# Softmax sums divided untransposed in groups of eight heads, the maxima's product outside the ring of banks, the shared expert's gate product in place

## The reference, cut to what matters

```python
# 16 heads of 16 channels; qc from x, kc and vc from the context
y  = softmax(causal(q @ k.T * scale)) @ v          # self attention
y += softmax(qc @ kc.T * scale) @ vc               # cross attention, added
x  = x + tanh(g0) * (y @ Wp + bp)                  # q, k, v, qc from layernorm(x)
h  = layernorm(x)
out = shared_expert(h) + sum over top 2 of 7 experts of w[e] * expert_e(h)
x  = x + tanh(g1) * out                            # expert: (silu(h @ g.T) * (h @ u.T)) @ d.T
```

## Time and profile before

| | µs |
|---|---|
| median of three runs (lowest, highest) | 1413.26 (1413.21, 1413.28) |
| the profiled execution | 1413.27 |
| its span, first to last instruction | 1411.5 |
| TensorE busy in the span | 1368.6 |
| VectorE busy | 880.9 |
| ScalarE busy | 727.3 |
| GpSimd busy | 365.4 |

### The profile page before, as it was taken

The page is one execution under the profiler, slowest core; times in us unless marked ns, Lnnn a source line. Parts: engine busy times, 40 slices in busy tenths (PEclk is TensorE's granted clock), DMA queues, the critical chain, the costliest instruction groups (busy, mean ns, idle before and its releaser), DMA issues.

```text
span 1411.5 us, 27301 instructions
## 1 busy us (share of the span) xinstructions
PE 1368.6 (97%) x7688; PEld 694.0 (49%) x7689; DVE 880.9 (62%) x1804; ACT 727.3 (52%) x1107; POOL 365.4 (26%) x743
## 2 busy tenths in 40 slices
PE   7988999999999999999999999989999999999997
PEld 4544333333333333333333333364556777777775
DVE  6776888888888888888888888653532222222221
ACT  4644667677777676767676767732210222222221
POOL 5655222222222222222222222200001232233232
PEclk9999999999999999999999999999999999999999
DMA  8754111111111111111111111057004122112111
GB/s 246 237 186 154 43 53 51 48 50 48 47 49 50 51 50 50 49 48 48 48 51 51 50 49 50 7 218 297 0 1 134 26 33 34 30 30 37 30 30 23
DMA packets 57711, 98.43 MB, mean 70 GB/s; under 512 B 7441, under 2 KB 42001, under 8 KB 56657
## 3 DMA queue, kind: packets, MB, share of 16 engines
q1 hardware_dynamic: 50384, 88.10, 18.8%
q0 software_dynamic: 7296, 9.97, 4.5%
HBM read 69.20 MB, written 28.58 MB: 69 GB/s over the span
## 4 chain that ended last, share of the span: by engine, by line
PE 88%; DMA 2%; DVE 2%; ACT 1%; issue 1%; POOL 1%; SPq 0%; POOLq 0%; ACTq 0%; DVEq 0%
PE ps L669 19%; PE ps L834 13%; PE ps L651 13%; PE ps L551 13%; PE ps L847 7%; PE ps L786 5%; PE ps L797 3%; PE ps L718 3%; PE ps L654 2%; PE ps L565 2%; PE ps L858 2%; DMA k_parts<-work 2%; PE ps L555 1%; PE ps L592 1%; PE ps L625 1%
## 5 line engine op out<-in xcount | busy, mean ns | idle before, releaser
L1242 DVE TENSOR_REDUCE mx<-ps 128x1 f32<-128x512 f32 (+1 forms) x832 | 515.1, 662 | 99.6 <-PE ps L551 69.3
L993 ACT ACTIVATE arena<-ps 128x1024 f32<-128x1024 f32 (+1 forms) x512 | 484.3, 995 | 138.7 <-PE ps L651 135.2
L669 PE MATMUL ps<-arena 128*32 128x512 f32 (+5 forms) x2432 | 290.9, 525 | 0.6 <-ACT arena L993 0.4
L551 PE MATMUL ps<-arena 96*128 96x512 bf16 x768 | 263.0, 382 | 7.3 <-DMA arena<-k_parts 2.9
L651 PE MATMUL ps<-arena 98*128 98x512 bf16 x832 | 264.4, 381 | 5.0 <-DMA arena<-rowst 4.9
L1144 POOL TENSOR_SCALAR_AFFINE_SELECT arena<-arena 128x128 f32<-128x128 f32 x256 | 74.8, 292 | 439.2 <-ACT arena L993 429.3
L834 PE MATMUL ps<-arena,work 128*128 x608 | 186.4, 460 | 0.6 <-issue 0.6
L551 PEld LDWEIGHTS ps<-arena 96*128 96x128 bf16 x768 | 74.1, 96 | 178.0 <-DVE mx L1242 103.2
L1520 DVE TENSOR_TENSOR work<-work,ps 128x352 f32<-128x352 f32 x76 | 39.6, 521 | 179.1 <-ACT work L1061 179.1
L834 PEld LDWEIGHTS ps<-arena,work 128*128 128x128 f32 x608 | 112.5, 190 | 57.4 <-issue 1.1
L1242 DVE TENSOR_REDUCE mneg<-ps 128x2 f32<-128x512 f32 (+2 forms) x192 | 112.4, 640 | 23.9 <-PE ps L561 23.4
(11 more groups left out here) (161 smaller groups left out, 1406.8 us busy)
## 6 DMA issues: line engine op xcount, KB each, us to landing
arena<-in_experts SPq DMA_DIRECT2D x8, 2176.0 KB, 12.2
arena<-k_parts SPq DMA_DIRECT2D x64, 198.1 KB
arena<-k_parts SPq DMA_DIRECT2D x64, 132.1 KB
arena<-q_parts SPq DMA_DIRECT2D x64, 96.0 KB
k_parts<-work SPq DMA_DIRECT2D x16, 300.0 KB, 5.2
q_parts<-work SPq DMA_DIRECT2D x12, 384.0 KB, 5.4
arena<-k_parts SPq DMA_DIRECT2D x64, 66.0 KB
arena<-q_parts SPq DMA_DIRECT2D x64, 64.0 KB
```

Of the source, the lines that this page charges most:

```text
L551: mm = pe.matmul(out, qx[:, qt * P:(qt + 1) * P], ks[0:KROWS, T + j * CHUNK:T + (j + 1) * CHUNK], start=True, stop=True)
L669: mm = pe.matmul(ps[32 * q:32 * q + VW, 6, b0:b1], vst[0:kn, r % VR, TT + kt if cross else kt, :], pr[0:kn, c0:c0 + b1 - b0], start=(phase ...
L993: act.activation(pr[:, c0:c0 + n], ps[:, 2 * (g % 2):2 * (g % 2) + 2, :].rearrange("p b n -> p (b n)")[:, 0:n], ACT.Exp, scale=SCALE).then ...
L1242: return dve.tensor_reduce(m, out, AX_X, ALU.max)
```

## The change

Three things are done.

- **Sums.** `norm`, `norm_out`, `cross_sums` and `head_output` are gone. After `sums_out`, SyncE stores the sums of each head to memory (`sums_store`, 256 KB). For each group of eight heads it loads the denominators spread over 128 partitions (`den_load`), and the numerators of eight heads stacked over 128 partitions (`num_load`), which is already the channels-first layout that the projection reads (`yT`, in the place of `xnT`). GpSimd adds (`den_sums`, `num_sums`), VectorE takes one reciprocal, it goes through memory to be repeated over the 16 channels (`recip_store`, `recip_load`), and GpSimd divides and adds (`outputs`). The loop's body has eight steps, not four. The 32 transposes before the projection go. The projection of sequences 0 and 1 waits for their groups alone; the first two gate-and-up chunks of the shared expert stand between the projections of sequences 1 and 2 and of 2 and 3.
- **Maxima.** Four of a step's `max` products belong to head u+1 and twelve to head u+2; 28 are made in the preparation. The transposing product stands behind `max` 6, ahead of group 3, writes to bank 6 and takes 128 columns of weights (`mcols`, zero beyond 16). It waits for `o_evac`; the first value phase, which writes to bank 6 next, waits for `rows_evac`. ScalarE copies `rowst` behind the exponential of group 2, and issues the DMA itself. The ring holds the maxima and two entries that are never written ("spare").
- **Gate product.** SiLU writes into `hT` and VectorE multiplies there; `sg` is gone. Head 3's stack moves to `shared`, the shared expert's weights are loaded from head 60 on, and the routed experts' loads stand behind all stores of `xn_rows`.

```diff
--- before.py
+++ after.py
...
-HALF = NMAX // 2
-MAXED = NMAX + HALF
+BACK = 4
+DONE = NMAX - BACK
+MAXED = NMAX + DONE
...
+        if g == 3:
+            out.append(("rows",))
...
         if g == 3:
-            out += [("values", 0), ("norm",)]
+            out += [("spare", 0), ("values", 0)]
         if g == 5:
-            out += [("rows",), ("values", 1)]
+            out += [("spare", 1), ("values", 1)]
...
-ENTRIES = [item for item in PE_ORDER if item[0] in ("max", "norm", "rows")]
+ENTRIES = [item for item in PE_ORDER if item[0] in ("max", "spare")]
...
+GH = P // D
+NGRP = NU // GH
+BEGUN = GH - 2
+TURNS = NGRP - 1
+DENS_IN, RECIP_IN, SUMS_IN, OUT_IN, RECIP_AT = 3, 4, 6, 7, 6
...
+    for u in range(BEGUN):
+        step(u, u % NR, u > 0, True, True)
+    with eng.Fori(0, TURNS) as i:
+        for h in range(GH):
+            step(i * GH + (BEGUN + h), (BEGUN + h) % NR, True, True, True, i, h)
...
+        o_parts = nc.dram_tensor("o_parts", (NU, P, T), F32, kind="Internal").ap()
+        recip_rows = nc.dram_tensor("recip_rows", (NGRP, 2, GH, T), F32, kind="Internal").ap()
...
+        kst.append(shared[:, 0:KSIZE])
+        qst.append(shared[:, KSIZE:KSIZE + QSIZE])
...
+        mcols = sb("mcols", [P, P], BF16)
...
+        rows_bank = ps[:, 6, 0:P]
...
+            def sums_store(v):
+                sp.wait_ge(S["o_evac"], v + 1)
+                sp.dma_start(o_parts[bass.ds(v, 1)].rearrange("a p t -> (a p) t"), osb).then_inc(S["o_written"], 16)
...
+            def den_load(j, h0=0, h1=GH):
+                sp.wait_ge(S["parts_free"], j + 1)
+                sp.wait_ge(S["o_written"], j * (16 * GH) + 16 * h1)
+                heads = o_parts[bass.ds(j * GH + h0, h1 - h0)]
+                for q in range(4):
+                    src = heads[:, VW * q + D:VW * q + D + 1, :].rearrange("u a (d t) -> (u a) d t", t=DW)
+                    sp.dma_start(den[h0 * D:h1 * D, q, :], src).then_inc(S["den_in"], 16)
...
+            def num_load(j, q, h0=0, h1=GH):
+                dst = [yT[:, bass.ds(j, 1), :].rearrange("p a t -> p (a t)"), *cross_num, self_num][q]
+                sp.dma_start(dst[h0 * D:h1 * D, :], o_parts[bass.ds(j * GH + h0, h1 - h0)][:, VW * q:VW * q + D, :]
+                             ).then_inc(S["num_in"], 16)
...
+            def recip_store(j):
+                sp.wait_ge(S["recip_done"], j + 1)
+                for s in range(2):
+                    sp.dma_start(recip_rows[bass.ds(j, 1), s, :, :].rearrange("a u (d t) -> (a u) d t", t=DW), recip[:, s, :]
...
+            def recip_load(j):
+                sp.wait_ge(S["recip_out"], j * 32 + 32)
+                for s, dst in enumerate((cross_recip, self_recip)):
+                    src = recip_rows[bass.ds(j, 1), s, :, :].rearrange("a u t -> (a u) t").unsqueeze(1)
+                    sp.dma_start(dst, src.to_broadcast([GH, D, T])).then_inc(S["recip_in"], 16)
...
+            def head(u, j=None, h=None, loads=True):
+                sp.wait_ge(S["qk_done"], u * NG + NG)
+                if loads:
+                    stack_loads(u + NR, (BEGUN + h if j is not None else u) % NR)
+                if h == 2:
+                    den_load(j)
+                    num_load(j, 0)
+                if h == 3:
+                    num_load(j, 1)
+                if h == 4:
+                    num_load(j, 2)
+                    num_load(j, 3)
+                if h == 5:
+                    recip_load(j)
+                sums_store(u)
+                if h == 3:
+                    recip_store(j)
...
+            for q, dst in enumerate([yT[:, NGRP - 1, :], *cross_num, self_num]):
+                sp.dma_start(dst[P - D:P, :], osb[VW * q:VW * q + D, :]).then_inc(S["num_in"], 16)
+            recip_store(NGRP - 1)
+            recip_load(NGRP - 1)
...
+                at -= RING if ENTRIES[at - RING][0] != "spare" else 2 * RING
+                before = ENTRIES[at]
+                step = u if at >= 0 else u - 1
...
+                v, piece, slot = (u + 1, c + DONE, r + 1) if c < BACK else (u + 2, c - BACK, r + 2)
...
-                pe.matmul(out[0:MROWS * 2 * TT, 0:P], mparts[:, :, :, :].rearrange("q m i t -> q (m i t)"), identb[:, :],
+                pe.matmul(out, mcols[:, :], identb[:, :],
...
-                            if prev:
+                            if nxt:
+                                pe.wait_ge(S["rows_evac"], u + 2)
+                            elif prev:
                                 pe.wait_ge(S["o_evac"], u)
                         values(u, r, item[1])
-                    elif item[0] == "norm" and prev:
-                        bank_free(u, "norm")
-                        norm(u)
                     elif item[0] == "rows" and nxt:
-                        bank_free(u, "rows")
-                        max_rows(u + 1, bank_of("rows"))
+                        if prev:
+                            pe.wait_ge(S["o_evac"], u)
+                        max_rows(u + 1, rows_bank)
...
-            def norm(u):
-                if isinstance(u, int) and u > 1:
-                    pe.wait_ge(S["norm_evac"], u - 1)
-                pe.wait_ge(S["o_evac"], u)
-                out = bank_of("norm")
-                for t in range(TT):
-                    mm = pe.transpose(out[:, t * P:(t + 1) * P], osb[:, t * P:(t + 1) * P], ident[:, :])
-                mm.then_inc(S["norm_mm"], 1)
...
-            for n in range(8):
-                b, k = divmod(n, 2)
-                if n >= 4:
-                    pe.wait_ge(S["y_freed"], n - 3)
-                layer_turn(ps[:, n % 4, :], b, k).then_inc(S["y_turned"], 1)
+            pe.wait_ge(S["max_red"], NU * NMAX - MAXED)
+            pe.wait_ge(S["rows_evac"], NU)
...
+                pe.wait_ge(S["y_done"], 2 * b + 2)
...
+                    if t == 2:
+                        pe.wait_ge(S["o_evac"], NU)
...
-            for b in range(B):
-                if b == B - 1:
-                    turn_xn(0)
-                project(b)
+            project(0)
+            project(1)
+            turn_xn(0)
             pe.wait_ge(S["shared_load"], 16)
-            shared_up(0)
+            shared_up(0, 0, 1)
+            project(2)
+            shared_up(0, 1, 2)
+            project(3)
+            shared_up(0, 2, IT)
...
-            def rows(v, out):
+            def rows(v, r, out):
                 act.wait_ge(S["rows_tr"], v + 1)
                 if not (isinstance(v, int) and v == 0):
                     act.wait_ge(S["rows_ready"], v * 16)
                 act.activation(rowst[:, :], out[0:MROWS * 2 * TT, 0:P], ACT.Copy).then_inc(S["rows_evac"], 1)
+                act.wait_ge(S["rows_evac"], v + 1)
+                act.dma_start(qst[r][KROWS:KROWS + MROWS, :, :].rearrange("p i t -> p (i t)"), rowst[:, :]
+                              ).then_inc(S["rows_ready"], 16)
...
                 act.wait_ge(S["pv_done"], u * NPH)
+                if not (isinstance(u, int) and u == 1):
+                    act.wait_ge(S["o_written"], u * 16 - 16)
                 act.activation(osb[:, :], ps[:, 6, :], ACT.Copy).then_inc(S["o_evac"], 1)
...
-                    if g == 3 and prev:
-                        norm_out(u)
-                    if g == 5 and nxt:
-                        rows(u + 1, bank_of("rows"))
+                    if g == 2 and nxt:
+                        rows(u + 1, (r + 1) % NR, rows_bank)
...
+            act.wait_ge(S["o_evac"], NU)
+            for q in range(4):
+                src = osb[VW * q + D:VW * q + D + 1, :].rearrange("a (d t) -> a d t", t=DW)
+                act.dma_start(den[P - D:P, q, :], src).then_inc(S["den_in"], 16)
...
+                    if it == 0 and tb >= 2:
+                        act.wait_ge(S["down_mm"], tb - 1)
+                    if it == 0 and tb == 1:
+                        act.wait_ge(S["first_rows"], 16 * (HT_TILES // TT))
+                    if k0 == 0:
+                        act.wait_ge(S["recip_out"], 32 * NGRP)
+                    if k0 == 2:
+                        act.wait_ge(S["den_in"], 64 * (NGRP + 2))
+                        act.wait_ge(S["num_in"], 64 * (NGRP + 2))
+                    if k0 == 3:
+                        act.wait_ge(S["y_done"], NGRP)
                     act.wait_ge(S["up_mm"], k0 + 1)
-                    if k0 >= 2:
-                        act.wait_ge(S["h_done"], k0 - 1)
-                    else:
-                        act.wait_ge(S["first_rows"], 16)
-                    act.activation(sg[0:m, k0 % 2, :], ps[0:m, 2 * (k0 % 2), :], ACT.Silu).then_inc(S["silu_done"], 1)
+                    act.activation(hT[tb % 2][0:m, it, :], ps[0:m, 2 * (k0 % 2), :], ACT.Silu).then_inc(S["silu_done"], 1)
...
-                if prev:
-                    cross_sums(u)
                 mask(u, 2, TT)
-                if prev:
-                    head_output(u)
-                    pool.wait_ge(S["y_done"], u)
+                if h == DENS_IN:
+                    den_sums(group)
```

(64 more changed lines are left out.)

208 lines of the change are left out of this document (81 added, 127 removed).

## The result

The changed kernel takes 1418.13 µs (median of six runs, 1416.87 to 1420.62), the kernel before 1413.24 in the same sessions (1412.99 to 1413.86). The ratio is 1.0037, 95% interval 1.0024 to 1.005: **slower by 5 µs**, where 1386 was forecast. The profiled execution has a span of 1415.9 µs (before 1411.5) and a granted clock of 0.981 (before 0.993).

The account below looks back on a forecast made before the run. TensorE was taken as the bound, at 12.28 µs a head. Gains of 18.9 (steps), 4 (start), 1.5 (heads 62 and 63) and 3 (tail) sum to 27.4, from 1413.27 to 1386 µs; range 1366 to 1405.

Parts of the forecast that it names:

- start of the steps, to the first evacuation: Before the first heads: `rowst`'s DMA no longer waits behind SyncE's stores; gain 4 µs, bounds 2 and 6.
- 61 heads: The steps: each gains 0.63 of TensorE's work less a 0.32 stall, 0.31 µs; 18.9 over 61 steps.
- heads 62 and 63: Last two heads: without `norm`, fewer maxima and no late `rowst`, 18.6 becomes 17.1; gain 1.5 µs, bounds 0 and 2.5.
- tail: Behind the last values: 44.2 µs against 47.2, the gate product shortening nothing; gain 3, bounds -1 and 8.
- What else moves, inside the steps: Inside the heads: moved work on SyncE, GpSimd, VectorE and the ring is off the path and costs nothing.
- The list of rivals: Hidden evacuation 1366 (0.18), dear ScalarE issue 1401 (0.17), slower (0.08), change not doing what it says (excluded).
- one slower case: ScalarE's DMA issue from 1.25 µs on eats all gains through group 3's late exponential; at 1.6, 1435 µs; chance 0.08.
- What would show it: Signs in the changed profile: period near 11.97, some 0.3 idle on TensorE; TensorE waiting mainly for VectorE or stacks overturns it.
- Stall before the first value phase: Each head: TensorE, ready at 1.84, waits for ScalarE's rows copy until 2.16; 0.32 µs, bounds 0.0 and 0.45.
- The cover of the DMA's issue: ScalarE's issue, 0.68 beside a cover of 0.8, delays group 3's exponential without TensorE waiting; cost nothing, bound 0.3 a head.
- TensorE's work: Each head: `norm` gone saves 0.48, a cheaper rows' product 0.13 to 0.15; about 0.63 µs, bounds 0.50 and 0.75.

Follow-up runs that it names:

- straight code: The changed kernel with VectorE's loop over groups of eight heads written out, no other engine's code differing: 1392.16 µs, ratio 0.9856 to the kernel before.
- The edit above: VectorE's loop written out in the changed kernel, and behind the heads ScalarE copies the first turned tiles before its second square root: 1388.71 µs, ratio 0.982.

## Why the prediction was wrong

It forecast 27.4 µs less; the profiled execution is 4.4 longer. By the evacuations' times (before: first 155.27, heads 61 and 63 at 904.39 and 922.92; after: 149.71, 909.28, 926.65; straight code: 149.59, 883.98, 901.35):

| gain, µs | predicted | changed kernel | straight code |
|---|---|---|---|
| start of the steps, to the first evacuation | 4 | 5.6 | 5.7 |
| 61 heads | 18.9 | -10.4 | 14.7 |
| heads 62 and 63 | 1.5 | 1.2 | 1.2 |
| tail | 3 | -0.7 | 0.4 |
| sum | 27.4 | -4.4 | 22.0 |

- **The step that failed** is "What else moves, inside the steps. Nothing of this is on the path". It went through SyncE, GpSimd, VectorE's reciprocals and the ring, and each of these was right: heads with the group's work take 12.04 like the others. It never asked what a loop body of eight heads does to the engine that runs it. VectorE's body grew from 166 to 316 instructions, and each turn then costs 3 µs on the engine that had been found to have slack. Slack counted per head hides little of one lump: 3.21 µs leave 2.52 of idle time on TensorE, 2.0 to 2.2 leave 1.2 to 1.4, and 3.8 leave 3.2. Six turns and three falls of the clock are 25.2 µs, the difference of the two right columns in the heads' row.
- **The list of rivals** had one slower case, an issue on ScalarE above 1.25 µs. The row is 0.62 to 0.63. The slower result came by a mechanism that was in none of the cases, so 0.08 for slower was the price of one mishap that was thought of, not of those that weren't. "What would show it" did name TensorE waiting for VectorE as what would overturn the account.
- **Stall before the first value phase**: 0.32 forecast, 0.31 measured, by the mechanism forecast. Two of its terms were off and cancelled in part: counted from the quarter's first product at 359.26 the copy ends 2.03 in (2.11 forecast), and TensorE starts 0.19 behind it (0.05 forecast, from another pair of rows); it would have been ready at 1.91, not 1.84. So the closeness of the number is partly luck. The cover of the DMA's issue held; its 0.89 for half a quarter should by its own terms have been 0.98, which only widens it.
- **TensorE's work**: 12.04 - 0.31 = 11.73, so 0.55 less than before and not 0.63, inside the bounds (0.50 to 0.75). That is the 4.2 µs by which the straight code falls short in the heads' row. Whether `norm` or the rows' product was over-sized was not told apart.
- **Start**: 5.6 for 4, inside 2 to 6. The first exponential came at 136.60 (forecast 136.3, before 139.97); the rest was slow first quarters that became short: before, the grant was 0.50 from 135.8 to 146.0, and in the changed kernel it stayed full. The number hangs on such falls: in the straight code the exponential came at 134.86, the grant fell for 6.8 µs, and the gain was 5.7.
- **Heads 62 and 63**: 1.2 for 1.5. Its own terms (sixteen exponentials at 0.95, two evacuations) add up to 16.4, not 17.1; between the evacuations it took 17.37 (before 18.53).
- **Tail**: 0.4 for 3 in the straight code. The forecast had sequence 0 "turned and copied" at 13.4 behind the last values, and named the copy's place behind sequence 1's deviations without pricing it: the first gate product starts 915.57 - 901.29 = 14.3 behind them, 3.50 of it idle, and the first chunk then takes 5.08 where 3.5 was forecast, at a grant of 0.50. The 0.9 and the 1.6 are 2.5 of the 2.6 that are missing. The forecast took the full clock through the tail; a fall of 6.8 µs (10.2 in the changed kernel, from 935.9) stood there instead. The edit above takes out 2.7 of the idle time, and nearly half of that is lost again at the low clock. Two small VectorE operations beside GpSimd's additions (1.26 µs each, from 932.10 and 933.50) also grew, in the changed kernel as in the straight code:

```profile
932.41 0.97 DVE L1307 TENSOR_SCALAR sd<-mv 128x4 f32<-128x4 f32 x1
933.87 2.01 DVE L1310 TENSOR_SCALAR shared<-x,mv,rs 128x256 f32<-128x256 f32 x4
```

Later ones of these lines take 0.17 and 1.38: 1.4 µs ahead of the turns that TensorE waits for, of the kind that the forecast had looked for inside the steps, where it did not occur.

## What to carry to other kernels

When a change lengthens a hardware loop's body, count the instructions of the body on every engine and compare with bodies that are known to turn for free; a lump on an engine with slack cost all but 0.6 to 0.8 µs of itself here, with three buffers between it and the engine that bounds the time. Look in the page for the instruction queue's packets and in the waits for a few long "issue" entries. And where a small copy gates the bounding engine, look first at what stands ahead of it in its engine's order: one exponential moved behind it was worth 17 µs.

## What the runs showed of the hardware

- On VectorE a loop of 166 or 248 instructions turned free, and one of 316, 330 or 494 left it idle for 2.0 to 3.4 µs a turn, with five or six packets on the instruction queue. TensorE's body in the changed kernel has 1526 instructions in the trace (matmuls and weight loads counted apart), and in the straight code its eighth heads are at most 0.04 µs longer than the others.
- The granted clock fell to 0.50 at three of six stalls of 2.2 to 2.8 µs (for 6.8, 10.2 and 10.2 µs), at all six of 3.2 (3.4 to 10.2), at two of four of 1.7 to 1.9 in the run with twelve heads a body (3.4 each), and at none of 1.2 to 1.4. Why it alternated in the changed kernel stays open.
- A DMA issued by ScalarE takes 0.62 µs of its time, and the next exponential starts 0.77 behind the copy.
